# A fused attention and expert block: statistics of x moved among the first scores, and the attention of the last batch as products over 32 rows

## The chip, the cores and the metric

One core of a Trainium2 chip. The metric is the time of the device for one execution of the whole program, in microseconds (us). The program is written engine by engine: TensorE (PE), VectorE (DVE), ScalarE (ACT), GpSimd (POOL) and SyncE (SP, which only issues transfers) each have a fixed list of instructions, and semaphores join the lists.

## The reference

Four batches of 512 tokens, 128 values each, all in float32. An attention layer and a layer of eight experts (two of them weighted for each token) each stand between two normalisations and are added to x.

```python
x = x + layernorm(attention(layernorm(x)))
x = x + layernorm(ffn(layernorm(x)))

# attention, by batch:
probs = softmax(q @ k.T / sqrt(128)); out = probs @ v
# ffn, by token:
cont = sigmoid(h @ W_enc + b_enc) @ W_s2c + b_s2c        # 128 -> 256 -> 64
gate = two largest of softmax(cont @ Wr + br), scaled to a sum of 1
moe  = sum over 8 experts e of gate[e] * (relu(cont @ W1[e] + b1[e]) @ W2[e] + b2[e])
out  = layernorm(sigmoid(moe @ W_c2s + b_c2s) @ W_dec + b_dec) * ln_g + ln_b
```

## The kernel before

The 512 tokens of a batch b lie as four tiles t of 128 rows. `scores(b, t)` makes one tile's 128x512 scores in one of the two PSUM banks `ps_s`. VectorE takes the row maximum (`row_max`), ScalarE the exponentials with their row sums (`exps`), TensorE turns the tile's probabilities in four 128x128 blocks through its array (`turn_probs`, into `ps_t`), ScalarE copies them out (`pT_out`), and TensorE multiplies them with v, four products to a tile (`attend`, into `ps_o`). The row sums are never divided out: a normalisation follows, and the sums only scale its epsilon (`attn_var`). ScalarE sums the squares of the attention's output (`attn_squares`), GpSimd takes the power -1/2 (`inverse_std`), VectorE adds to x (`mid_stats`, which also takes the statistics of the sum) and normalises (`mid_norm`).

The experts follow: `encode`, `to_cont`, `route` on TensorE; `router_top`, `router_index`, `router_gates` on VectorE; the gates go through DRAM and come back spread over all partitions (`gate_out`, then SP's fetches); `hidden_pair` makes two experts' hidden layers, `gate_hidden` on VectorE does relu and gate for one expert, `expert_out` is the second product, `to_spikes` and `decode` the way back. `x_stats` and `x_norm` are statistics and normalisation of the input. Six small instructions on VectorE split a bias into bfloat16 pieces (`b_dec_hi` to `b_dec_stack`); `scaled_weights` centres the decoder's weights; both feed only the decoder.

The batches are pipelined by hand: while VectorE and ScalarE do the softmax of one batch, TensorE has the experts of an earlier one between. Nothing but these lists sets the order. Each engine takes its instructions strictly in turn, so an instruction that waits holds back all behind it.

Of the kernel before, what the change touches and what calls it, by code (L numbers as in the profile page):

```python
# [17 lines left out]
def attention_moe_block(  # L18
# [25 lines left out]
    out_dram = out.rearrange("b (p t) d -> b p t d", t=T)  # L44
    gates_dram = [nc.dram_tensor(f"gates{b}", [E, S], F32) for b in range(B)]

    with ExitStack() as ctx:
# [69 lines left out]
        x_out = sb("x_out", [P, B, T, D])  # L117
# [69 lines left out]
        ps_o = psum("ps_o", [P, 2, S])  # L187
        ps_c = psum("ps_c", [P, 2, S])
# [38 lines left out]
        def decoded_bank(b, t):  # L227
# [1329 lines left out]
```

## Time and profile before

| | us |
|---|---|
| three runs: median (lowest to highest) | 131.16 (130.88 to 131.32) |
| the profiled execution, its own time | 130.91 |
| span in its trace | 129.0 |
| TensorE busy | 118.7 (92% of the span) |
| VectorE busy | 94.4 (73%) |
| ScalarE busy | 58.8 (46%) |
| GpSimd busy | 33.8 (26%) |

The span runs from the first to the last instruction; 1.9 us of the execution's time lie around it. Busy time of TensorE counts overlapping products once, and also the time in which a product's end is still on its way through the array. A float32 product that isn't a transpose stands in the trace as two records.

### The profile page before, as it was taken

What the parts mean: (1) busy time and instruction counts of PE and PEld (TensorE: products, weight loads), DVE (VectorE), ACT (ScalarE), POOL (GpSimd) and SP (SyncE); (2) the same over time, 40 slices, a digit from 0 to 9 for tenths busy, and PEclk for the clock granted to TensorE, in tenths of its full rate; (3) what the DMA queues carried; (4) which work ended last, traced back from release to release, by engine and by line L of the source; (5) the groups of instructions that cost most, each with busy time, mean ns of one, the idle gap of its engine ahead of it and who ended that gap; (6) DMA issues with size and microseconds to landing.
All of it is one profiled execution on the core that took longest, in us unless ns stands there. A gap on an engine that the chain in (4) does not pass through costs nothing.

```text
span 129.0 us, 2501 instructions
## 1 busy us (share of the span) xinstructions
PE 118.7 (92%) x815; PEld 80.1 (62%) x815; DVE 94.4 (73%) x400; ACT 58.8 (46%) x173; POOL 33.8 (26%) x70
## 2 busy tenths in 40 slices
PE   6999999999999989999999999999998899998920
PEld 2556786878645767754575994657565455864910
DVE  0858537698989874788957168966889999389672
ACT  1647765556837575204666542053713003903620
POOL 4423503325231162220000132230081043330551
PEclk9999999999999999999999999999999999999998
DMA  3558800000000019700000198000019749720022
GB/s 113 132 121 227 234 18 3 0 0 3 0 5 0 0 50 324 290 8 0 0 0 0 41 293 329 3 0 0 8 48 319 299 138 323 276 86 0 4 79 81
DMA packets 9370, 12.42 MB, mean 96 GB/s; under 512 B 3169, under 2 KB 5998, under 8 KB 9358
## 3 DMA queue, kind: packets, MB, share of 16 engines
q1 hardware_dynamic: 8254, 12.08, 28.5%
q10 hardware_dynamic: 1104, 0.20, 0.8%
q8 instruction: 6, 0.10, 0.3%
q14 instruction: 6, 0.05, 0.1%
HBM read 11.16 MB, written 1.11 MB: 95 GB/s over the span
## 4 chain that ended last, share of the span: by engine, by line
PE 54%; DVE 23%; issue 8%; POOL 7%; ACT 3%; DMA 2%; POOLq 1%; DVEq 0%
PE ps_t L942 10%; POOL rstd L431 7%; PE ps_s L804 6%; PE ps_o L829 6%; PE ps_s L918 5%; PE ps_c L918 4%; DVE stats L1172 3%; PE ps_o L858 3%; PE ps_t L816 3%; DVE x_out L1366 2%; DMA x_in<-in_L_attn_x 2%; DVE xn L1184 2%; PE ps_o L918 2%; PE ps_a L769 2%; DVE neg_max L1200 2%
## 5 line engine op out<-in xcount | busy, mean ns | idle before, releaser
L431 POOL TENSOR_TENSOR rstd<-var_eps,minus_half 128x2 f32<-128x2 f32 (+1 forms) x33 | 25.4, 771 | 88.9 <-DVE var_eps L1177 47.3
L829 PEld LDWEIGHTS ps_o<-v,probsT 128*128 128x128 f32 x128 | 15.6, 191 | 4.6 <-ACT probsT L546 4.1
L829 PE MATMUL ps_o<-v,probsT 128*128 128x128 f32 x128 | 17.5, 279 | 0.4 <-ACT probsT L546 0.3
L942 PE MATMUL ps_t<-gated,w 128*64 128x256 f32 x128 | 17.0, 389 | 0.9 <-DVE gated L1286 0.8
L804 PE MATMUL ps_s<-xnT,yT 128*128 128x512 f32 x32 | 16.0, 596 | 0.1
L541 ACT ACTIVATE probs<-ps_s,neg_max 128x512 f32<-128x512 f32 x16 | 11.0, 687 | 11.1 <-DVE neg_max L1200 11.0
L1200 DVE TENSOR_REDUCE neg_max<-ps_s 128x1 f32<-128x512 f32 x16 | 10.9, 689 | 5.0 <-PE ps_s L804 4.9
L942 PEld LDWEIGHTS ps_t<-gated,w 128*64 128x64 f32 x128 | 8.0, 136 | 8.8 <-DVE gated L1286 4.2
L1286 DVE SCALAR_TENSOR_TENSOR gated<-ps_s,b_minus,gate_all 128x512 f32<-128x512 f32 x14 | 9.9, 744 | 1.9 <-PE ps_s L918 1.9
L546 ACT ACTIVATE probsT<-ps_t 128x512 f32<-128x512 f32 x16 | 9.5, 594 | 2.6 <-PE ps_t L816 2.4
L562 ACT ACTIVATE spikes<-ps_o,bias_half 128x512 f32<-128x512 f32 x6 | 4.1, 687 | 13.5 <-PE ps_o L858 13.4
L816 PE MATMUL ps_t<-ident,probs 128*128 128x128 f32 x64 | 9.8, 276 | 0.2 <-ACT probs L541 0.2
L816 PEld LDWEIGHTS ps_t<-ident,probs 128*128 128x128 f32 x64 | 7.3, 141 | 4.2 <-ACT probs L541 2.4
L1286 DVE SCALAR_TENSOR_TENSOR gated<-ps_c,b_minus,gate_all 128x512 f32<-128x512 f32 x12 | 8.4, 743 | 2.0 <-PE ps_c L918 2.0
L583 ACT ACTIVATE moeT<-ps_t 128x256 f32<-128x256 f32 x4 | 1.5, 384 | 14.5 <-PE ps_t L942 14.5
L918 PE MATMUL ps_s<-cont,w 64*128 64x256 f32 x56 | 7.9, 401 | 0.0
L804 PEld LDWEIGHTS ps_s<-xnT,yT 128*128 128x128 f32 x32 | 5.2, 191 | 2.7 <-issue 2.4
L1212 DVE SCALAR_TENSOR_TENSOR var_eps<-square_sum,eps_term 128x2 f32<-128x2 f32 x8 | 1.3, 165 | 7.1 <-ACT squares L552 6.9
L918 PE MATMUL ps_c<-cont,w 64*128 64x256 f32 x48 | 6.3, 380 | 0.0
L1219 DVE SCALAR_TENSOR_TENSOR x_mid<-ps_o,rstd,x_in 128x128 f32<-128x128 f32 x16 | 4.8, 343 | 2.0 <-POOL rstd L431 2.0
L918 PEld LDWEIGHTS ps_s<-cont,w 64*128 64x128 f32 x56 | 4.8, 186 | 2.1 <-issue 1.5
L1184 DVE TENSOR_SCALAR xn<-x_in,mean_var,rstd 128x128 f32<-128x128 f32 x16 | 5.2, 375 | 1.2 <-POOL rstd L431 0.9
(207 smaller groups left out, 218.6 us busy)
## 6 DMA issues: line engine op xcount, KB each, us to landing
gate_all<-gates SPq DMA_DIRECT2D x12, 512.0 KB, 6.0
gate_all<-gates SPq DMA_DIRECT2D x8, 256.0 KB, 3.6
x_in<-in_L_attn_x SPq DMA_DIRECT2D x3, 256.0 KB, 3.6
w<-in_L_ffn_W SPq DMA_DIRECT2D x3, 256.0 KB, 4.4
out<-x_out SPq DMA_DIRECT2D x3, 256.0 KB, 2.0
x_in<-in_L_attn_x SPq DMA_DIRECT2D x2, 128.0 KB, 2.5
out<-x_out SPq DMA_DIRECT2D x2, 128.0 KB, 1.7
w_enc<-in_L_ffn_W_enc SPq DMA_DIRECT2D x1, 128.0 KB, 2.7
```

Source lines behind the costliest of these rows:

```text
L431: nc.gpsimd.tensor_tensor(rstd[part], var_eps[part], minus_half[:, t0:t1], ALU.pow).then_inc(g_rstd[n], 1)
L541: nc.scalar.activation(probs[:, b % 2, t], ps_s[:, t % 2], ACT.Exp, bias=neg_max[:, b % 2, t:t + 1], accum_out=prob_sum[:, b % 2, t:t + 1] ...
L546: nc.scalar.activation(probsT[:, b % 2, t], ps_t[:, :].rearrange("p (k q) -> p k q", k=T), ACT.Identity).then_inc(a_pT, 1)
L804: nc.tensor.matmul(ps_s[:, t % 2], yT[:, b % 2, t * P:(t + 1) * P], xnT[:, b % 2], start=True, stop=True).then_inc(pe_s, 1)
L816: mm = nc.tensor.transpose(ps_t[:, k * P:(k + 1) * P], probs[:, b % 2, t, k * P:(k + 1) * P], ident[:, :])
L829: mm = nc.tensor.matmul(attn_out(t), probsT[:, b % 2, t, k], v[:, b % 2, k], start=(k == 0), stop=(k == T - 1))
L918: mm = nc.tensor.matmul(hidden_banks(b, e)[:, h], w1[half, e], cont[half, b % 2], start=True, stop=True)
L942: mm = nc.tensor.matmul(ps_t[h * M:(h + 1) * M, 0:SH], w2[:, e], gated[:, e, h * SH:(h + 1) * SH], start=False, stop=(e == E - 1))
L1184: nc.vector.tensor_scalar(result(t), source(t), mean_var[:, n, b % 2, t, 0:1], inv(n, b, t), ALU.subtract, ALU.mult).then_inc(done, 1)
L1200: nc.vector.tensor_reduce(neg_max[:, b % 2, t:t + 1], ps_s[:, t % 2], AX_X, ALU.max, negate=True).then_inc(v_max, 1)
L1219: nc.vector.scalar_tensor_tensor(x_mid[:, b, t], attn_out(t), inv(LN_ATT, b, t), x_in[:, b, t], ALU.mult, ALU.add).then_inc(v_mid, 1)
L1286: nc.vector.scalar_tensor_tensor(token_halves(gated[:, e]), hidden_banks(b, e), b1_minus[:, e:e + 1], token_halves(gate_all[:, b % 2, e]), ...
```

## The change

It has two parts and a new order around them.

1. `x_stats(2)` and `x_stats(3)` move from the middle of the attention of batches 1 and 2 to the first scores; the `x_norm` of both moves forward too. GpSimd's `inverse_std(LN_X, ...)` moves with them.
2. For batch 3 `turn_probs` and `pT_out` are gone. VectorE turns each probability tile in 32x32 blocks (`turn_blocks`: four transposes of 128x512). A block turned this way stays in its own 32 partitions, so the attention is summed as products over 32 rows: `attend_last` makes 64 products of 32 rows, 128 columns of weights and 129 columns of v, one partition group i of 32 after the other, each group with its own PSUM bank. For this v must be there for every key block in all four groups of partitions: SP writes v of batch 3 to DRAM and reads it back four times (`v_all`). The 129th column of v is one, so that the row sums come out of the products; the exponentials of batch 3 no longer sum. `yT` of batch 3 is written with its tokens permuted, so that the result has the rows in x's order. ScalarE copies the result out once (`att_out`, 128x516), and everything after reads the copy. The statistics of x_mid for batch 3 are squares summed on ScalarE (`mid_square`) about x's mean, in place of VectorE's bn_stats.
3. Order: `turn_x(2)` and `project_y(2)` stand earlier, the product behind `b_dec_sum` later; the six bias instructions move from batch 1's attention to behind the first two `turn_blocks`; all four scores of batch 3 now stand among the last expert products of batch 0, and `decode(0, ...)` is done before `attend_last`; `scaled_weights` stands behind the turned blocks; in front of the third expert round `z_stats` and `z_centre` of batch 0 stand ahead of `router_top(2)`, and the first two `gate_hidden(2, ...)` ahead of the last steps of the router of batch 3. `x_out` is gone: the result goes into `x_in`.

The diff, cut; the third piece stands in `hidden_pair`.

```diff
 for b in range(B):
+    if b == 1:
+        sp.wait_ge(g_v_ones, 1)
+        sp.wait_ge(a_v, B)
+        sp.dma_start(v_dram.ap(), v[:, (B - 1) % 2].rearrange("p t d -> p (t d)")).then_inc(d_v_out, 16)
+        sp.wait_ge(d_v_out, 16)
+        for i in range(T):
+            sp.dma_start(v_all[32 * i:32 * (i + 1)].rearrange("a j t d -> a j (t d)"),
+                         v_dram.ap().rearrange("(j a) x -> a j x", j=T)).then_inc(d_v_all, 16)
...
+def attend_last():
+    pe.wait_ge(v_blocks, T)
+    pe.wait_ge(d_v_all, 16 * T)
+    pe.wait_ge(v_mid, T * (B - 1))
+    pe.wait_ge(v_logit, 2)
+    pe.wait_ge(a_c2s, HC)
+    pe.wait_ge(v_gated, E)
+    for j in range(S // 32):
+        for i in range(T):
+            rows = slice(32 * i, 32 * (i + 1))
+            mm = nc.tensor.matmul(ps_oc[:, i, 0:D + 1], blocks[rows, j].rearrange("p t r -> p (t r)"),
+                                  v_all[rows, j % T, j // T], start=(j == 0), stop=(j == S // 32 - 1))
+    mm.then_inc(pe_o, 1)
...
     if b < 2:
+        if b == 1:
+            pe.wait_ge(a_exp, T * B)
         if p == 1:
+            if b == 1:
+                pe.wait_ge(a_att, 1)
+            pe.wait_ge(v_bdec, 1)
...
+def att_out():
+    act.wait_ge(pe_o, 2 * B - 1)
+    nc.scalar.activation(att[:, :, :], ps_oc[:, :, 0:D + 1], ACT.Identity).then_inc(a_att, 1)
+def mid_square(h):
+    b = B - 1
+    act.wait_ge(v_mid, T * b + TH * (h + 1))
+    for t in range(TH * h, TH * (h + 1)):
+        nc.scalar.activation(squares[:, b % 2, t], x_mid[:, b, t], ACT.Square, scale=-1.0,
+                             bias=mean_var[:, LN_X, b % 2, t, 0:1],
+                             accum_out=mid_square_sum[:, t:t + 1]).then_inc(a_mid_square, 1)
...
+def turn_blocks(t):
+    dve.wait_ge(a_exp, T * (B - 1) + t + 1)
+    dve.wait_ge(pe_o, 4)
+    nc.vector.transpose(blocks[:, :, t], probs[:, (B - 1) % 2, t]).then_inc(v_blocks, 1)
```

Three places show how rows move. First, TensorE's list from the last expert products of batch 0 (`ps_t<-gated,w`) to the first of batch 1. Before:

```order
L942 MATMUL ps_t<-gated,w 64x256 x8
L873 MATMUL ps_a<-spikes,w_s2c 64x256 x4
L954 MATMUL ps_c<-moeT,w_c2s 128x256 x4
L885 MATMUL ps_o<-w_r,cont 128x8 x4
L844 MATMUL ps_a<-ident,hn 128x128 x4
L816 MATMUL ps_t<-ident,probs 128x128 x4
L804 MATMUL ps_s<-xnT,yT 128x512
L829 MATMUL ps_o<-v,probsT 128x128 x4
L816 MATMUL ps_t<-ident,probs 128x128 x4
L804 MATMUL ps_s<-xnT,yT 128x512
L829 MATMUL ps_o<-v,probsT 128x128 x4
L816 MATMUL ps_t<-ident,probs 128x128 x4
```

The same place after the change (`xnT,yT` are the scores, `ident,hn` is `turn_h(2)`, `w_dec,spikes` is `decode(0, ...)`, `cont,w` is `hidden_pair(1, ...)`):

```order
L1010 MATMUL ps_t<-gated,w 64x256 x4
L852 MATMUL ps_s<-xnT,yT 128x512
L1022 MATMUL ps_oc<-moeT,w_c2s 128x256 x4
L852 MATMUL ps_s<-xnT,yT 128x512
L902 MATMUL ps_a<-ident,hn 128x128 x4
L1028 MATMUL ps_t<-b_dec_stack,ones_bf 128x512
L1068 MATMUL ps_t<-w_dec,spikes 128x128 x8
L889 MATMUL ps_oc<-v_all,probsT 128x129 x64
L983 MATMUL ps_s<-cont,w 128x256 x4
L983 MATMUL ps_oc<-cont,w 128x256 x4
```

The four turns and four attentions that alternated with other work are one run of 64 products, which needs all four tiles.

Second, VectorE's list between the third row maximum of batch 0 and the first of batch 1. Before:

```order
L1200 TENSOR_REDUCE neg_max<-ps_s 128x1
L1395 BN_STATS dec_stats<-w_dec_raw 128x6 x2
L1396 BN_STATS dec_stats<-b_dec_all 128x6
L1200 TENSOR_REDUCE neg_max<-ps_s 128x1
L1400 BN_AGGR dec_mean<-dec_stats 128x2 x2
L1401 BN_AGGR dec_mean<-dec_stats 128x2
L1208 SCALAR_TENSOR_TENSOR eps_term<-prob_sum 128x2
```

After:

```order
L1265 TENSOR_REDUCE neg_max<-ps_s 128x1
L1492 BN_STATS dec_stats<-w_dec_raw 128x6 x2
L1493 BN_STATS dec_stats<-b_dec_all 128x6
L1237 BN_STATS stats<-x_in 128x6 x4
L1240 BN_AGGR mean_var<-stats 128x2 x4
L1242 TENSOR_SCALAR var_eps<-mean_var 128x4
L1265 TENSOR_REDUCE neg_max<-ps_s 128x1
L1498 BN_AGGR dec_mean<-dec_stats 128x2 x2
L1499 BN_AGGR dec_mean<-dec_stats 128x2
L1237 BN_STATS stats<-x_in 128x6 x4
L1240 BN_AGGR mean_var<-stats 128x2 x4
L1242 TENSOR_SCALAR var_eps<-mean_var 128x4
```

Each of the two blocks of nine statistics instructions of batches 2 and 3 now stands on one side of the fourth row maximum.

Third, VectorE's list behind the turned blocks of batch 3 (`x_mid<-att` is `mid_add`, `gated` is `gate_hidden(1, ...)`); before, the first `gated` of this round stood directly behind `z<-ps_a,g_all`:

```order
L1432 TENSOR_SCALAR b_centred<-b_all,scaled_mean 128x128
L1278 SCALAR_TENSOR_TENSOR eps_term<-att 128x2
L1282 SCALAR_TENSOR_TENSOR var_eps<-square_sum,eps_term 128x2
L1294 SCALAR_TENSOR_TENSOR x_mid<-att,rstd,x_in 128x128 x2
L1278 SCALAR_TENSOR_TENSOR eps_term<-att 128x2
L1282 SCALAR_TENSOR_TENSOR var_eps<-square_sum,eps_term 128x2
L1383 SCALAR_TENSOR_TENSOR gated<-ps_s,b_minus,gate_all 128x512 x2
L1294 SCALAR_TENSOR_TENSOR x_mid<-att,rstd,x_in 128x128 x2
L1383 SCALAR_TENSOR_TENSOR gated<-ps_oc,b_minus,gate_all 128x512
```

`gate_hidden(1, 0)` now has the whole first half of the attention's normalisation ahead of it on its engine.

## Rows read from the trace of the kernel before

**Rows 1.** The page, top and part 1: engine, busy us, share, instructions.

```profile
span 129.0 us, 2501 instructions
PE 118.7 (92%) x815; PEld 80.1 (62%) x815; DVE 94.4 (73%) x400; ACT 58.8 (46%) x173; POOL 33.8 (26%) x70
```

**Rows 2.** One window: length, busy us of PE, PEld, DVE, ACT, POOL; clock; DMA.

```profile
76.50:88.40 11.90, 11.89 (x86) 6.73 (x85) 9.41 (x27) 4.00 (x16) 2.78 (x4) 1.00 0.30 110
```

**Rows 3.** TensorE's timeline, from route(0) to hidden_pair(0, 0): start, us, what, [idle before].

```profile
36.58 0.62 PE L885 MATMUL ps_c<-w_r,cont 64*128 64x8 f32 x8
...
51.93 1.14 PE L918 MATMUL ps_s<-cont,w 64*128 64x256 f32 x8
52.90 1.03 PE L918 MATMUL ps_c<-cont,w 64*128 64x256 f32 x8
```

**Rows 4.** VectorE's timeline, the places that the moved statistics leave and take.

```profile
16.49 0.69 DVE L1200 TENSOR_REDUCE neg_max<-ps_s 128x1 f32<-128x512 f32 x1 [1.77 <-PE ps_s L804]
...
19.11 0.16 DVE L1212 SCALAR_TENSOR_TENSOR var_eps<-square_sum,eps_term 128x2 f32<-128x2 f32 x1 [1.67 <-ACT squares L552]
...
33.92 0.22 DVE L1435 CAST b_dec_hi<-b_dec_sum 128x128 bf16<-128x128 f32 x1
...
35.50 0.16 DVE L1208 SCALAR_TENSOR_TENSOR eps_term<-prob_sum 128x2 f32<-128x2 f32 x1
...
43.40 0.86 DVE L1172 BATCH_NORM_STATS2 stats<-x_in 128x6 f32<-128x128 f32 x4
```

**Rows 5.** TensorE's timeline, the attention of batch 3 and what surrounds it.

```profile
62.03 1.95 PE L942 MATMUL ps_t<-gated,w 128*64 128x256 f32 x16
...
65.74 0.51 PE L885 MATMUL ps_o<-w_r,cont 64*128 64x8 f32 x8
66.18 0.66 PE L844 MATMUL ps_a<-ident,hn 128*128 128x128 f32 x4
...
70.71 1.16 PE L829 MATMUL ps_o<-v,probsT 128*128 128x128 f32 x8 [0.29 <-ACT probsT L546]
...
73.25 1.06 PE L829 MATMUL ps_o<-v,probsT 128*128 128x128 f32 x8
74.14 0.60 PE L816 MATMUL ps_t<-ident,probs 128*128 128x128 f32 x4
74.58 1.06 PE L1002 MATMUL ps_a<-w_dec,spikes 128*128 128x128 f32 x8
...
76.52 1.13 PE L918 MATMUL ps_s<-cont,w 64*128 64x256 f32 x8
```

**Rows 6.** Groups by line and form: count, busy us, mean ns of one.

```profile
L1200 DVE TENSOR_REDUCE neg_max<-ps_s 128x1 f32<-128x512 f32 x16 | 10.9, 689 | 5.0 <-PE ps_s L804 4.9
L1277 DVE STREAM_TRANSPOSE gate_blocks<-gate 128x32 f32<-128x32 f32 x4 | 0.8, 212 | 0.1
L1263 DVE TENSOR_SCALAR e_sum<-e 128x4 f32<-128x4 f32 x4 | 0.7, 162 | 0.0
```

**Rows 7.** ScalarE's and VectorE's timelines, batch 3's first half normalised, then gated hidden layers.

```profile
72.83 0.27 ACT L552 ACTIVATE squares<-ps_o 128x128 f32<-128x128 f32 x1
...
73.56 0.16 DVE L1212 SCALAR_TENSOR_TENSOR var_eps<-square_sum,eps_term 128x2 f32<-128x2 f32 x1 [2.34 <-ACT squares L552]
74.53 0.61 DVE L1219 SCALAR_TENSOR_TENSOR x_mid<-ps_o,rstd,x_in 128x128 f32<-128x128 f32 x2 [0.81 <-POOL rstd L431]
...
77.70 0.75 DVE L1286 SCALAR_TENSOR_TENSOR gated<-ps_s,b_minus,gate_all 128x512 f32<-128x512 f32 x1 [1.02 <-PE ps_s L918]
```

**Rows 8.** TensorE's timeline from route(2) on, and its last group.

```profile
88.40 0.62 PE L885 MATMUL ps_o<-w_r,cont 64*128 64x8 f32 x8
...
97.04 1.13 PE L918 MATMUL ps_o<-cont,w 64*128 64x256 f32 x8 [0.61 <-DVE logits L1232]
...
100.46 1.31 PE L942 MATMUL ps_t<-gated,w 128*64 128x256 f32 x8 [0.84 <-DVE gated L1286]
...
106.72 1.14 PE L918 MATMUL ps_s<-cont,w 64*128 64x256 f32 x8
```

More of the change, by code:

```diff
@@ new lines, in _ @@
+            pe.wait_ge(v_wdec, 8)
+            pe.wait_ge(v_logit, 1)
+            for c in range(HC):
+                mm = nc.tensor.matmul(ps_c[:, 0, 0:D], ones[:, :], w_dec[:, c], start=(c == 0), stop=(c == HC - 1))
+            mm.then_inc(pe_bdec, 1)
+            turn_probs(2, 0)
+            scores(2, 2)
+            attend(2, 0)
+            turn_probs(2, 1)
+            turn_h(1)
+            scores(2, 3)
+            attend(2, 1)
+            turn_probs(2, 2)
+            turn_x(3)
+            attend(2, 2)
@@ new lines, in _ @@
+            turn_probs(2, 3)
+            project_y(3)
+            attend(2, 3)
+            project_v(3)
+            hidden_pair(0, 0)
+            hidden_pair(0, 1)
+            expert_biases(0)
+            for e in range(4):
+                expert_out(0, e)
+            hidden_pair(0, 2)
+            hidden_pair(0, 3)
+            encode(1, 0)
+            encode(1, 1)
+            scores(3, 0)
+            scores(3, 1)
+            to_cont(1)
+            expert_out(0, 4)
+            expert_out(0, 5)
@@ new lines, in _ @@
+            route(1)
+            expert_out(0, 6)
+            expert_out(0, 7)
+            scores(3, 2)
+            to_spikes(0)
+            scores(3, 3)
+            turn_h(2)
+            for t in range(T):
+                decode(0, t)
+            attend_last()
+            hidden_pair(1, 0)
+            hidden_pair(1, 1)
+            expert_biases(1)
+            for e in range(4):
+                expert_out(1, e)
+            hidden_pair(1, 2)
+            hidden_pair(1, 3)
+            encode(2, 0)
@@ L1491, in _ @@
             gate_hidden(1, 7)
-            dec_var(0, 0)
             z_scale(0, 0)
+            z_stats(0, 0)
+            z_centre(0)
             router_top(2)
@@ L1496, in _ @@
             router_gates(2)
-            z_stats(0, 0)
-            z_centre(0)
             z_add(0, 0)
@@ L1503, in _ @@
             router_index(3)
-            router_gates(3)
-            for e in range(6):
+            router_weights(3)
+            gate_hidden(2, 0)
+            gate_hidden(2, 1)
+            router_blocks(3)
+            for e in range(2, 6):
                 gate_hidden(2, e)
```

360 lines of the change are left out of this document (178 added, 182 removed).

## The prediction

> **What bounds the kernel now.** I read the page first, then the windows, then the timelines of the engines. TensorE is busy for 118.7 of 129.0 us [rows 1], and between 76.5 and 88.4 without a gap, at the full clock (1.00, the level of 2.4 GHz) [rows 2]. So the end moves with TensorE: by the products that it no longer makes, and by the waits that it gains or loses. A busy TensorE hides small waits, however. Each step has a pace that shows where nothing holds it: four attention products (eight records) take 0.89 us (73.25 to 74.14), four turns 0.44 (74.14 to 74.58) [rows 5]. From `route(0)` at 36.58 to `hidden_pair(0, 0)` at 51.93 it takes 15.35 us [rows 3] for work worth some 12.7: four scores of 0.86, four turns, four attentions, and 4.0 us of projections, turns of x and h, and routing. About 2.6 us are late answers of VectorE and ScalarE. In the attention of batch 3 (66.18 to 76.52) 10.3 us hold 5.3 us of turning and attending [rows 5].
>
> All times below are in the frame of this trace. The profiled execution took 130.91 us, 1.9 more than its span; the median of the runs shown is 131.16, so I add 0.25 at the end.
>
> **First statistics.** Each `x_stats` is 1.35 us of VectorE (43.40 on: four of bn_stats, four aggregates, one more) [rows 4]. VectorE idles 1.77 us ahead of the fourth row maximum of batch 0 and 1.67 us ahead of 19.11, waiting for squares [rows 4]. If x has landed, both blocks fit there and cost nothing; if that cover were gone, each would push a row maximum by up to 1.35. Landing is my estimate: the loads for batches 2 and 3 are issued at 10.5 and 13.4 us by SP and land in some 3.6, so by 14.1 and 17.0, while VectorE gets to them at 14.7 and 17.4. The norm of batch 2 (1.1 us) goes into a similar gap near 23.5.
>
> What leaves the middle: 1.35 us ahead of the last row maximum of batch 2, 1.35 at 29, and the six bias instructions, 33.92 to 35.50, 1.6 us [rows 4]. I followed the lists from `route(0)`: with y of batch 2 projected earlier, scores(2, 2) starts 0.9 earlier, the last row maximum 1.0 earlier, turn_x(3) 1.2, and `hidden_pair(0, 0)` at 50.5 in place of 51.93, after the 0.44 of the product behind b_dec_sum, which now lies in this stretch. **Term 1: -1.4.** Bounds: 0 (a single late answer remains) and -2.2 (2.6 less 0.44).
>
> **The attention of batch 3.** From 62.03 TensorE has left: experts 4 to 7 (1.8), to_cont 1.0, route 0.44, two scores 1.7, to_spikes 1.0, turn_h 0.5, decode(0) 2.0. That is 8.4 us and replaces 14.5 less 5.3 of turns and attentions (some 0.8 of the 14.5 was waiting, 0.29 of it at 70.71 [rows 5]).
>
> The price of `attend_last` is not in the trace. A record of 128 columns over the full array comes every 111 ns (0.89 over 8) [rows 5]; 128 records in a row would be 14.2 us. But products over 64 rows run two at a time: `hidden_pair` makes 8 records of 256 columns in 0.97 us (51.93 to 52.90) [rows 3], 121 ns each, when the full array's pace would be 222. Their weight loads go in pairs too: in route 8 records, each with 128 columns of weights, take 0.44 us (65.74 to 66.18), 55 ns each [rows 5]. So with pairs only it is 7.2 us, with four at a time 32 steps of 112 ns, 3.6. The list rotates over the four groups, each with its own bank, as route's and hidden_pair's do over two, so I take 3.6 and 0.2 for its start: 3.8. The Trainium skill weighs against this: "TensorE: Matmul & The Clock Gate", Part 3 (measured speedup), gives 3.07 times for four products of 32 rows, not four. By that it would be an estimated 14.2/3.07 = 4.6 us, 0.8 more; no row here shows four.
>
> What it waits for: the last `turn_blocks`. A 128x512 reduction on VectorE takes 689 ns. The transposes seen are 128x32, 212 ns, against 162 for an operation of 4 columns [rows 6]: 50 ns for 28 columns more would be 1.8 ns a column, 1.0 us for 512; if it streams as the reduction does, 0.69. I take 0.69, nearest in size (in a row 0.6, since starts overlap ends); the other end adds 0.3 twice before the router of batch 1 and twice after, 1.2 in all. The Trainium skill, "Vector Engine (DVE) Microarchitecture Reference", 3.8, has the transpose sustain one element per cycle per lane, which would be the short one.
>
> Followed through, still without term 1: blocks 0 and 1 and the bias pieces end at 65.7, router_top(1) to its weights at 67.7, row maximum 68.3, router_blocks 69.2, row maximum 69.85, exponential 70.55, block 3 done 71.3. `decode(0)` waits for the second `spike2(0, ...)`, now behind an exponential, and runs 69.8 to 71.8; TensorE idles 1.3 before it. The transposes are thus just hidden. The attention runs 71.8 to 75.6, against hidden_pair(1, 0) at 76.52 [rows 5]. **Term 2: -0.9.** v_all's data (1 MB, issued after 51) lands by 62 and isn't late.
>
> **Behind the attention.** Here a wait is added. hidden_pair(1, 1) waits for att_out (0.6 us on ScalarE plus 0.2 to be noticed), about covered by the 0.97 of hidden_pair(1, 0). But gate_hidden(1, 0) is now queued behind attn_var(3, 0), mid_add(3, 0) and attn_var(3, 1), and expert_out(1, 0), with all of TensorE's list behind it, waits for it. From the attention's end: 0.85 copy, 0.5 squares (before: first square at 72.83, var_eps at 73.56), 1.0 from var_eps to x_mid (73.56 to 74.53), 0.6 x_mid, 0.2 attn_var, then 0.7 for the gate [rows 7]: expert_out(1, 0) starts 4.1 after the end. Before, gate_hidden started at 77.70, 1.2 after 76.52 [rows 5, 7]. Then VectorE paces the first four experts (four gates of 0.67, 0.6 of mid_add, small ones): expert 3 at 6.85, hidden_pair(1, 2) 7.3 to 8.25, and the encoders, turn_h(3), the last experts and to_cont(2) follow at their pace, with route(2) 14.25 after the end. Before it was 11.88 (76.52 to 88.40) [rows 5, 8]. **Term 3: +2.35.** Nothing but the end of the DVE list hides it, since VectorE is filled by scaled_weights only until just before. Its bounds: 0 if the first experts were as quick as before, +3.5 if POOL's powers for LN_MID hold mid_norm(3, 1) another 1.1.
>
> **The last third.** route(2) comes at -1.4 - 0.9 + 2.35 = 0.05 after 88.40. Behind it VectorE had 97.04 held up by 0.61 and 100.46 by 0.84 [rows 8]. With z_stats and z_centre (2.1 us) taken out from between routers 2 and 3, the logits of batch 3 are taken as soon as they exist: hidden_pair(2, 2) starts 0.35 earlier. With router_blocks(3) behind gate_hidden(2, 0), expert_out(2, 0) starts 1.0 earlier. The router's last steps (0.8) then delay gates 2 to 5 of this round, and of the 1.0 some 0.7 to 0.75 are left at 106.72 [rows 8]. From there to its last product TensorE waits little, so the rest shifts. **Term 4: -0.75** (0 to -1.4, all of both waits).
>
> Sum: -1.4 - 0.9 + 2.35 - 0.75 = -0.7. 130.91 - 0.7 = 130.2, plus 0.25: **130.4 us** against 131.16.
>
> **Rivals.**
> - *The four row groups do not pack as two do* (their loads or the order of issue are shared). Pairs only: +3.4, 133.8, chance 0.10. The middle between pairs and four, 5.4 us: +1.6, 132.0, chance 0.07. For it: no four are seen here. Against: every pair in the trace overlaps in loads and products. By the skill's 3.07 it would be +0.8, 131.2, between this and the forecast. Beyond 4.5 us of attention the change no longer pays.
> - *Slow transposes*, the one that ends on the other side by one mechanism on VectorE: 1.0 us each puts the attention 1.2 later, nothing takes it back, 131.6; chance 0.15. It decides from 0.2 us over my price per transpose.
> - *The front gains nothing*, because another late answer (ScalarE's copies between TensorE's steps) takes the place of VectorE's: +1.4 on the sum, 131.8; chance 0.13. For it: ScalarE copies between nearly all of TensorE's steps here. Against: each step that I followed had its predecessors.
> - *The hand-over is cheaper than term 3* by a microsecond: 129.4; chance 0.10.
> - The forecast, 130.4 with 129.7 to 131.0 as its own range: chance 0.45.
>
> **How the numbers follow.** 0.3% (about what a measurement of this kernel can tell) is 0.4 us: faster means below 130.77, slower above 131.55. Faster: 0.10 + 0.38 of the forecast's 0.45 + 0.03 of the front's = 0.51. Slower: 0.17 of the packing + 0.08 of the transposes + 0.06 of the front = 0.31. The same: 0.07 + 0.07 + 0.04 of these three (forecast, transposes, front) = 0.18. For the range I leave out the pairs (0.10) and the ends of the others: 129.1 to 132.5, which takes in both prices of the transpose and the middle of the packing.
>
> **What would show it.** attend_last as 128 records within 3.6 to 4 us; transposes of 0.7; `hidden_pair(0, 0)` near 50.5; route(1), ahead of the last scores, near 62.6; the attention ending near 74.2; TensorE idle for about 1.7 us ahead of expert_out(1, 0), and smaller gaps behind it with VectorE named; route(2) near 88.4; hardly any wait for logits at 96.7. The prediction is wrong if the attention's records come more than 35 ns apart, if row_max(0, 3) starts later than 16.6 because x had not landed, if SP's transfers of v stand in front of gates that are needed, or if TensorE's gaps behind the attention let its clock fall to the lower level (1.2 GHz), of which the trace of before has no case until its products are over.

## The result

The changed kernel takes 134.28 us (median of 6 runs, 132.26 to 136.04) against 131.03 (130.85 to 132.65): slower, and outside my range of 129.1 to 132.5. Its ratio to the kernel before is 1.0159, 95% interval 1.0095 to 1.0223 (the ratio leaves out runs more than 1.5% above the fastest). The profiled execution took 134.0, with a span of 132.2.

The top of its page, part 1, and the row of part 2 with the granted clock in 40 slices, answer to [rows 1]:

```profile
span 132.2 us, 2668 instructions
PE 121.2 (92%) x895; PEld 79.6 (60%) x895; DVE 94.6 (72%) x396; ACT 58.8 (45%) x174; POOL 33.7 (26%) x71
...
PEclk9999999999999999999999999599999999999996
```

The 5 in the 26th slice is new: in the middle of the program TensorE ran at half its clock for a while. Three windows of the changed kernel, from the attention's end on (length, busy us of PE, PEld, DVE, ACT, POOL, clock, DMA share, GB/s), answer to [rows 2]:

```profile
78.96:80.96 2.00, 0.68 (x6) 0.20 (x4) 1.32 (x5) 0.86 (x6) 1.01 (x2) 1.00 0.98 397
80.96:84.96 4.00, 3.56 (x16) 1.12 (x16) 3.55 (x11) 1.05 (x6) 2.04 (x4) 0.64 0.26 101
84.96:88.96 4.00, 4.00 (x23) 2.48 (x22) 2.57 (x6) 0.67 (x1) 2.72 (x8) 0.94 0.00 0
```

TensorE works only 0.68 of 2 us, waiting for gates; then the granted clock is 0.64 and 0.94 on the mean of two windows in which it is busy. By these two rows it is at the lower of its two levels, 1.2 GHz, for 3.4 us.

TensorE's timeline of the changed kernel (start, us, what, [idle before]); from its third row on it answers to [rows 3, 5, 8]:

```profile
9.72 2.21 PE L852 MATMUL ps_s<-xnT,yT 128*128 128x512 f32 x4
...
17.15 1.02 PE L852 MATMUL ps_s<-xnT,yT 128*128 128x512 f32 x2
...
53.13 1.14 PE L983 MATMUL ps_s<-cont,w 64*128 64x256 f32 x8
...
71.18 0.38 PE L1028 MATMUL ps_t<-b_dec_stack,ones_bf 128*128 128x512 bf16 x1 [0.77 <-ACT spikes L639]
...
73.28 3.85 PE L889 MATMUL ps_oc<-v_all,probsT 32*128 32x129 f32 x128
77.06 1.13 PE L983 MATMUL ps_s<-cont,w 64*128 64x256 f32 x8
...
81.25 1.69 PE L1010 MATMUL ps_t<-gated,w 128*64 128x256 f32 x8 [1.61 <-DVE gated L1383]
...
92.25 0.61 PE L945 MATMUL ps_oc<-w_r,cont 64*128 64x8 f32 x8
...
109.94 1.14 PE L983 MATMUL ps_s<-cont,w 64*128 64x256 f32 x8
```

And the same places at the start of the kernel before:

```profile
8.32 1.88 PE L804 MATMUL ps_s<-xnT,yT 128*128 128x512 f32 x4
...
15.43 1.02 PE L804 MATMUL ps_s<-xnT,yT 128*128 128x512 f32 x2
```

Three things stand in these rows. The first scores already come at 9.72 instead of 8.32 and take 2.21 instead of 1.88, though no instruction of TensorE's was changed up to there: the products run at half pace until about 10.4 us (the first scores take 0.33 us more, which is some 0.7 us at half pace behind 9.72). The attention itself is 3.8 us long (73.28 to 77.06), as costed. And `route(2)` stands at 92.25, 15.2 us behind the attention's end, where it was 11.88 [rows 5, 8].

VectorE behind the attention answers to [rows 7]:

```profile
77.83 0.16 DVE L1278 SCALAR_TENSOR_TENSOR eps_term<-att 128x2 f32<-128x2 f32 x1 [1.65 <-ACT att L587]
78.63 0.16 DVE L1282 SCALAR_TENSOR_TENSOR var_eps<-square_sum,eps_term 128x2 f32<-128x2 f32 x1 [0.64 <-ACT squares L604]
79.60 0.61 DVE L1294 SCALAR_TENSOR_TENSOR x_mid<-att,rstd,x_in 128x128 f32<-128x128 f32 x2 [0.81 <-POOL rstd L458]
...
80.44 1.41 DVE L1383 SCALAR_TENSOR_TENSOR gated<-ps_s,b_minus,gate_all 128x512 f32<-128x512 f32 x2
```

And two groups by line and form, to [rows 6]:

```profile
L889 PE MATMUL ps_oc<-v_all,probsT 32*128 32x129 f32 x128 | 3.9, 274 | 0.0
...
L1289 DVE STREAM_TRANSPOSE probsT<-probs 128x512 f32<-128x512 f32 x4 | 2.8, 706 | 0.3
```

A transpose of 128x512 takes 706 ns, close to the 0.69 that I took and far from 1.0.

### The profile page after: what moved, and what is told of

It is laid out like the page before. It is cut to its first block, busy times and chain, and to the rows that moved or that the text cites. A ratio compares the mean times of both kernels' runs of the same rounds, so it can differ in the third digit from the quotient of the medians.

```text
span 132.2 us, 2668 instructions
## 1 busy us (share of the span) xinstructions
PE 121.2 (92%) x895; PEld 79.6 (60%) x895; DVE 94.6 (72%) x396; ACT 58.8 (45%) x174; POOL 33.7 (26%) x71
## 4 chain that ended last, share of the span: by engine, by line
PE 69%; DVE 14%; ACT 5%; issue 4%; POOL 3%; DMA 2%; POOLq 1%; ACTq 0%; DVEq 0%
PE ps_t L1010 9%; PE ps_s L852 8%; PE ps_oc L873 7%; PE ps_oc L918 6%; PE ps_s L983 5%; PE ps_oc L983 4%; PE ps_t L862 4%; PE ps_oc L889 3%; POOL rstd L458 3%; PE ps_a L825 2%; ACT probs L577 2%; PE ps_a L835 2%; DMA w_qkv<-in_L_attn_Wk 2%; PE ps_t L1068 2%; DVE neg_max L1265 2%
## 5 line engine op out<-in xcount | busy, mean ns | idle before, releaser
L1383 DVE SCALAR_TENSOR_TENSOR gated<-ps_oc,b_minus,gate_all 128x512 f32<-128x512 f32 x18 | 12.6, 741 | 2.1 <-PE ps_oc L983 2.1
L873 PE MATMUL ps_oc<-v,probsT 128*128 128x128 f32 x96 | 13.1, 279 | 0.2 <-ACT probsT L582 0.2
L873 PEld LDWEIGHTS ps_oc<-v,probsT 128*128 128x128 f32 x96 | 11.7, 192 | 2.7 <-ACT probsT L582 2.7
L614 ACT ACTIVATE spikes<-ps_oc,bias_half 128x512 f32<-128x512 f32 x8 | 5.5, 688 | 13.6 <-PE ps_oc L918 13.5
L983 PE MATMUL ps_oc<-cont,w 64*128 64x256 f32 x72 | 9.5, 388 | 0.3 <-DVE logits L1321 0.3
L862 PEld LDWEIGHTS ps_t<-ident,probs 128*128 128x128 f32 x48 | 5.4, 141 | 4.3 <-ACT probs L577 2.5
L918 PE MATMUL ps_oc<-hT,w_enc 128*128 128x512 f32 x16 | 7.8, 612 | 0.0
L983 PEld LDWEIGHTS ps_oc<-cont,w 64*128 64x128 f32 x72 | 6.6, 187 | 1.9 <-issue 0.4
L862 PE MATMUL ps_t<-ident,probs 128*128 128x128 f32 x48 | 7.3, 276 | 0.3 <-ACT probsT L582 0.3
L582 ACT ACTIVATE probsT<-ps_t 128x512 f32<-128x512 f32 x12 | 7.1, 592 | 0.8 <-PE ps_t L862 0.6
```

What stands on the lines that cost most here:

```text
L582: nc.scalar.activation(probsT[:, b % 2, t], ps_t[:, :].rearrange("p (k q) -> p k q", k=T), ACT.Identity).then_inc(a_pT, 1)
L614: nc.scalar.activation(spikes[:, b % 2, c], enc_bank(b, c), ACT.Tanh, bias=bias_half[:, c:c + 1], scale=0.5).then_inc(a_enc, 1)
L862: mm = nc.tensor.transpose(ps_t[:, k * P:(k + 1) * P], probs[:, b % 2, t, k * P:(k + 1) * P], ident[:, :])
L873: mm = nc.tensor.matmul(attn_out(t), probsT[:, b % 2, t, k], v[:, b % 2, k, 0:D], start=(k == 0), stop=(k == T - 1))
L918: nc.tensor.matmul(enc_bank(b, c), w_enc[:, c * P:(c + 1) * P], hT[:, b % 2], start=True, stop=True).then_inc(pe_enc, 1)
L983: mm = nc.tensor.matmul(hidden_banks(b, e)[:, h], w1[half, e], cont[half, b % 2], start=True, stop=True)
```

## The experiments

Five points cut each trace into stretches that can be compared whatever the start did: `scores(0, 3)`, `hidden_pair(0, 0)`, `hidden_pair(1, 0)` (the attention's end), `route(2)`, and `decode_scaled`'s first product with `w_z`. Times in us, each the difference of two starts on TensorE's timeline:

| trace | scores(0, 3) at | to hidden_pair(0, 0) | to hidden_pair(1, 0) | to route(2) | to decode_scaled |
|---|---|---|---|---|---|
| before | 15.43 | 36.50 | 24.59 | 11.88 | 32.91 |
| changed, first | 17.15 | 35.98 | 23.93 | 15.19 | 32.28 |
| changed, rerun (a1) | 15.20 | 35.99 | 23.93 | 14.39 | 32.91 |
| zeros in the gap (a2) | 15.05 | 35.98 | 23.93 | 14.75 | 33.24 |
| gates first (a3) | 15.67 | 35.98 | 23.93 | 13.55 | 33.39 |
| statistics back (b1) | 15.32 | 35.98 | 23.93 | 14.39 | 32.69 |
| old last third (b2) | 15.34 | 35.98 | 23.93 | 14.39 | 32.75 |
| gates of batch 1 sent early (d2) | 15.51 | 35.80 | 23.93 | 12.15 | 33.19 |
| no fetch, changed (f1) | 15.70 | 35.99 | 23.94 | 15.73 | 32.29 |
| no fetch, best order (f2) | 15.47 | 35.79 | 23.94 | 12.63 | 32.35 |

Among kernels with the same order there, the first two stretches repeat to 0.01 us. The others vary, by the clock and by a transfer, as the runs show.

**a1_again: nothing changed.** 

> The changed kernel, unaltered. Its six runs so far spread from 132.26 to 136.04, in step with their mean granted clock (0.988 to 0.967), and its trace has 3.4 us at 1.2 GHz behind the attention and reaches full pace of the products at 10.4 us instead of 4.8. Theory (the clock): the times fall into levels about 1.7 us apart, by how many such stretches a run has; the mean granted clock goes down by 0.013 with each (3.4 us at half of 132), and the late start, which the mean clock does not show, is chance: in this trace it can come at 4.8 or at 10.4. Rival (the schedule itself is slower): times within 0.5% at whatever clock.

133.45 us (131.89 to 135.38), ratio 1.0155 (1.0079 to 1.0231). This trace has neither the lower clock in the middle nor the late start, and the execution took 131.89, 1.0 above the profiled one of before. It is the schedule by itself. From the stretches: -0.23 at the start, -0.51, -0.66, +2.51, 0.00, in all +1.11 on TensorE. The first trace has +1.72, -0.52, -0.66, +3.31, -0.63, in all +3.22. The mean clock told of the middle (0.968 to 0.988), but levels 1.7 us apart were not to be seen: one run took 135.30 us at 0.986, which neither the clock in the middle nor one late start accounts for. Two executions of the kernel before are like it (134.25 and 134.39 at 0.990 and 0.989); they stay unexplained.

**a2_fill: products of zeros in the gap.** 

> Products of zeros into a free bank, eleven of 128 x 512 bf16, stand where TensorE waits for the gates behind the attention (seven ahead of expert_out(1, 0), four between the experts); nothing else is changed. Clock theory: TensorE has no gap there, the granted clock stays 1.00 until the last products, every run has the mean clock of 0.985 or more, and the median falls by 1.3 to 2 us, to 132.3 to 133. Rival 1 (the attention over 32 rows, not the gap, lowers the clock): the drop stays, the time stays 134 or gets worse. Rival 2 (the drop costs nothing, as VectorE paces the experts): the clock holds and the time stays within 0.4 us.

```diff
 expert_biases(1)
+fill(7)                       # matmul(ps_o[:, 0], zeros[:, 0:P], zeros)
 for e in range(4):
     expert_out(1, e)
+    fill((1, 2, 1, 0)[e])
```

132.42 us (132.36 to 133.85), ratio 1.0140 (1.0073 to 1.0206). No run had a mean clock under 0.987, where the changed kernel had 0.967 to 0.980 in 7 of 12. So it is the gap that brings the lower clock; d1 below shows it from the other side. The trace shows the price of the zeros too: `route(2)` 14.75 behind the attention's end, 0.36 more than in a1.

**a3_gates: four gates ahead of the norm.** 

> VectorE's list behind the attention only: gate_hidden(1, 0) to (1, 3) ahead of mid_add(3, 0), with both attn_var(3, ...) between the second and third gate. My step (the hand-over, +2.35 us, is there because the gates are queued behind the norm of batch 3): expert_out(1, 0) starts about 1.9 us after the attention's end instead of 4.2, route(2) within 12.5 us of it instead of 15.2, and the time falls by 2 to 3 us, to 131 to 132. With the gap smaller the clock should hold as well. Rival (the norm of batch 3, now later, becomes the late one at turn_h(3)): TensorE waits as long there and route(2) stays near 14.5.

```diff
+gate_hidden(1, 0)
+gate_hidden(1, 1)
 attn_var(3, 0)
-mid_add(3, 0)
 attn_var(3, 1)
-gate_hidden(1, 0)
-gate_hidden(1, 1)
-mid_add(3, 1)
 gate_hidden(1, 2)
-mid_var(0)
 gate_hidden(1, 3)
+mid_add(3, 0)
+mid_add(3, 1)
+mid_var(0)
 dec_var(0, 0)
```

131.61 us (130.25 to 133.97), ratio 1.0007 (0.9968 to 1.0047). `expert_out(1, 0)` starts 2.4 behind the end instead of 4.2, so the queue on VectorE is the cause of that first wait. But `route(2)` gains only 0.84 of the 2.51. TensorE and then VectorE in that kernel:

```profile
77.99 1.03 PE L1010 MATMUL ps_t<-gated,w 128*64 128x256 f32 x8
80.12 1.31 PE L1010 MATMUL ps_t<-gated,w 128*64 128x256 f32 x8 [1.10 <-DVE gated L1383]
...
85.80 0.66 PE L902 MATMUL ps_a<-ident,hn 128*128 128x128 f32 x4 [0.52 <-DVE hn L1312]
```

```profile
79.32 1.41 DVE L1383 SCALAR_TENSOR_TENSOR gated<-ps_oc,b_minus,gate_all 128x512 f32<-128x512 f32 x2 [0.60 <-DMA gate_all<-gates]
...
101.08 0.75 DVE L1383 SCALAR_TENSOR_TENSOR gated<-ps_s,b_minus,gate_all 128x512 f32<-128x512 f32 x1 [1.02 <-DMA gate_all<-gates]
```

The next late thing is the transfer of the rows of gates (VectorE's first row here), and then the norm, for which TensorE waits 0.52 (the rival, in part). VectorE's second row lies behind `route(2)`, where the rows are late as well.

**a4_unpacked: one row group after the other.** 

> attend_last with its two loops exchanged: the 32 products of one row group, then those of the next, each with its own bank as before. If the four groups overlap because their products alternate, none does now: 128 records at 111 ns, 14.2 us for the attention instead of 3.8, and the time near 144. If the order doesn't matter: 3.8 us and 134.

```diff
-for j in range(S // 32):
-    for i in range(T):
+for i in range(T):
+    for j in range(S // 32):
```

148.51 us. The attention on TensorE's timeline, then three windows inside it:

```profile
71.58 20.58 PE L889 MATMUL ps_oc<-v_all,probsT 32*128 32x129 f32 x128
```

```profile
72.00:76.00 4.00, 4.00 (x41) 4.00 (x40) 2.42 (x13) 1.14 (x8) 0.00 (x0) 1.00 0.79 222
...
77.30:80.00 2.70, 2.70 (x19) 2.70 (x18) 0.00 (x0) 0.00 (x0) 0.00 (x0) 0.50 0.65 264
80.00:85.00 5.00, 5.00 (x26) 5.00 (x26) 0.00 (x0) 0.00 (x0) 0.00 (x0) 0.50 0.01 5
```

At the full clock the records come every 111 ns, as said. But TensorE, busy without a gap inside the attention, was put to the lower clock 5.7 us into the attention and stayed there to its end: 20.5 us instead of 14.2. Alternating groups make 128 records in 3.78 us, 29.5 ns each, 3.8 times the pace of one group at full clock.

**b3_pairs: two row groups at a time.** 

> attend_last for two row groups at a time: the 64 products of groups 0 and 1 alternating, then those of 2 and 3. One group at a time took 111 ns a record at full clock and fell to 1.2 GHz after 5.7 us. If groups overlap as far as they alternate: 64 steps of 112 ns, 7.2 us, at full clock; the attention is then 3.4 longer than the 3.78 of four. If the array counts as busy only by the rows in use, the clock falls inside it or just behind, and it takes 8 or more; time 137 to 139.

```profile
71.28 7.08 PE L890 MATMUL ps_oc<-v_all,probsT 32*128 32x129 f32 x128
```

134.92 us. 7.0 us to the next product, as costed, at full clock. Groups overlap as far as they alternate.

**b1_stats_back: the statistics of term 1 put back.** 

> The changed kernel with x_stats(2), x_norm(2), x_stats(3) and x_norm(3), and POOL's powers for them, back at their old places among batches 1 and 2; TensorE's and ScalarE's new order stays. In the rerun of the changed kernel the stretch from scores(0, 3) at 15.20 to hidden_pair(0, 0) at 51.19 took 35.99 us, before 36.50: a gain of 0.5 where I had forecast 1.4. My step (VectorE's statistics were the late answers, and something took back 0.9): the stretch gets 0.9 to 1.6 us longer than 35.99, and the time rises by as much. Rival (row_max(2, 2) behind the router's steps of batch 0, at 42.60 in both kernels, and ScalarE's copies of the turned probabilities hold this stretch): it stays within 0.4 of 35.99.

```diff
-x_stats(2)
 row_max(0, 3)
 ...
-x_stats(3)
 attn_var(0, 0)
 ...
 row_max(2, 2)
+x_stats(3)
 row_max(2, 3)
+x_norm(3)
```

133.0 us (131.8 to 134.36), and the stretch is 35.98, the same to 0.01: the moved statistics are worth nothing. My term 1 is wrong, and the rival holds. The last two row maxima of batch 2 on VectorE, in the kernel before:

```profile
42.80 0.68 DVE L1200 TENSOR_REDUCE neg_max<-ps_s 128x1 f32<-128x512 f32 x1
...
45.01 0.69 DVE L1200 TENSOR_REDUCE neg_max<-ps_s 128x1 f32<-128x512 f32 x1 [0.26 <-PE ps_s L804]
```

And in the rerun (a1), with the waits of TensorE's weight loads for ScalarE's copies between 36 and 52 us (us in all, times, longest):

```profile
42.60 0.68 DVE L1265 TENSOR_REDUCE neg_max<-ps_s 128x1 f32<-128x512 f32 x1
...
44.69 0.69 DVE L1265 TENSOR_REDUCE neg_max<-ps_s 128x1 f32<-128x512 f32 x1 [1.40 <-PE ps_s L852]
```

```profile
PEld ps_oc L873 <- ACT probsT L582: 2.7, 4, 0.8
```

The third row maximum, behind the router's steps, comes 27.4 us behind `scores(0, 3)` in both. The fourth comes 0.1 earlier, where I had forecast 1.0: the time that the statistics left became a wait of VectorE for TensorE's scores. TensorE's loads wait 2.7 us for the copies there (2.3 before). That the copies hold the stretch fits this; no run made them faster. The 0.5 us that the stretch did gain comes with the new order of the lists around it, whose parts were not taken apart.

**b2_old_tail: VectorE's order of term 4 undone.** 

> The changed kernel with the old order of VectorE's last third: z_stats(0, 0) and z_centre(0) behind the router of batch 2, and the router of batch 3 undivided ahead of gate_hidden(2, 0). My step: from route(2) to hidden_pair(3, 1) it takes 18.3 us, as before, instead of 17.7 in the first trace of the changed kernel; expert_out(2, 0) 12.0 behind route(2) instead of 11.0. The rerun, however, took 18.33 for the stretch, with three waits of VectorE for the rows of gates (gate_all), 0.9 us in all. Rival (the new order only moves VectorE ahead of the transfer of these rows): no waits for gate_all here, and the stretch is 18.3 in any case, so the order is worth 0 to 0.7 by how quick the transfer is.

```diff
+router_top(2), router_index(2), router_gates(2)
 z_stats(0, 0)
 z_centre(0)
-router_top(2), router_index(2), router_gates(2)
 ...
-router_weights(3)
-gate_hidden(2, 0), gate_hidden(2, 1)
-router_blocks(3)
-for e in range(2, 6):
+router_gates(3)
+for e in range(6):
```

133.6 us (131.86 to 136.39). `expert_out(2, 0)` comes 11.87 behind `route(2)` instead of 11.0, and still the whole stretch is 32.75, between the two of the changed kernel. VectorE waited for no rows until gate 6 (0.75). In the rerun it had waited three times:

```profile
100.74 0.75 DVE L1383 SCALAR_TENSOR_TENSOR gated<-ps_s,b_minus,gate_all 128x512 f32<-128x512 f32 x1 [0.29 <-DMA gate_all<-gates]
...
103.71 1.41 DVE L1383 SCALAR_TENSOR_TENSOR gated<-ps_oc,b_minus,gate_all 128x512 f32<-128x512 f32 x2 [0.16 <-DMA gate_all<-gates]
...
105.69 1.41 DVE L1383 SCALAR_TENSOR_TENSOR gated<-ps_s,b_minus,gate_all 128x512 f32<-128x512 f32 x2 [0.42 <-DMA gate_all<-gates]
```

**f1_no_fetch and f2_no_fetch_best: the fetch taken away.** 

> The changed kernel, in which SP fetches no rows of gates for batches 2 and 3: their experts are weighted with the rows of batches 0 and 1, which are still there (that part of the result is left out). If the fetch is what took term 4 back, VectorE waits nowhere for gate_all behind route(2), the stretch from route(2) to the last product group takes 32.3 us or less, against 32.91 in the kernel before, and the median falls by 0.3 to 1.0 from 133.45 to 134.28. If something else on VectorE paces it, the stretch stays at 32.9.

> The same left out of d3_gates1_fill, whose 12 runs stood in two heaps, 129.8 to 130.1 and 130.9 to 131.7. If the late rows of batches 2 and 3 make the second heap, it is gone: all runs but late starts at or below 130.1, within 0.3 of each other. If the heaps stay, they come from elsewhere (the rows of batch 1, or the start).

```diff
 sp.wait_ge(d_gate_out[b], 16)
 if b >= 2:
-    sp.wait_ge(v_gated, E * (b - 1))
-    sp.wait_ge(pe_moe, b - 1)
+    continue
```

f1: 131.91 us (131.31 to 133.11), with 32.29 for the last stretch. The kernel before has no wait of VectorE for the rows behind `route(2)` in its trace, so this is about the order's own worth, -0.62 against 32.91: term 4 (-0.75) was nearly right. The fetch takes nothing of it in the first trace of the changed kernel and all of it in the rerun, and in a2 and a3, with the same order there, 0.3 and 0.5 more than all. f1's ten runs also price the clock: five with a mean clock of 0.990 or more stand at 131.3 to 131.6, five at 0.978 to 0.980 at 132.3 to 133.1, 1.3 us higher on the mean. f2: 129.66 us, ratio 0.9893 (0.9882 to 0.9904); ten of 12 runs lie between 129.46 and 129.92. d3's second heap (below) is gone, so the late rows, or `gateT` that is fetched with them, made it.

**c3_before_gap and d1_before_gap_long: a gap behind the old attention.** 

> The kernel before, with four additions on 128 x 512 put ahead of gate_hidden(1, 0) on VectorE, whose result nobody reads: expert_out(1, 0) comes 2.0 us later and TensorE waits about 1.7 us, as in the changed kernel, but behind the old attention over 128 rows. Theory (any gap of this length there can bring the lower clock): a part of the runs, a third to two thirds, have 3.4 us at 1.2 GHz, with a mean clock under 0.985 and a time 0.8 to 1.7 above the rest; the rest near 133. Rival (the attention over 32 rows is needed for it, as in the run with one group at a time, where the clock fell while it ran): no run under 0.985, all within 0.5 of 133 or 1.6 above with a late start.

> The kernel before with six additions ahead of gate_hidden(1, 0) instead of four: TensorE's gap behind the old attention over 128 rows becomes about 2.4 us, against 1.1 with four and 1.6 in the changed kernel. If a gap of this length is enough to bring the lower clock, a good part of the runs has 3.4 us of it (mean clock under 0.985) and spreads up by 1 to 2 us from 133.5. If the 32-row attention ahead of the gap has a part in it, no run is under 0.985, as with four.

```diff
 dec_scale(0, 0)
+for k in range(4):                     # d1: range(6)
+    tensor_tensor(idle, x_in[:, 0], x_in[:, 0], ALU.add)
 gate_hidden(1, 0)
```

c3: 132.22 us (131.54 to 133.67), no run of 7 under 0.985; its gap was only 1.1 us. d1: 134.35 us (133.37 to 135.52), 5 of 6 runs at 0.976 to 0.981. Its trace (TensorE, then a window):

```profile
81.90 3.62 PE L944 MATMUL ps_t<-gated,w 128*64 128x256 f32 x16 [2.54 <-DVE gated L1288]
```

```profile
82.00:84.00 2.00, 2.00 (x10) 0.92 (x12) 2.00 (x4) 0.00 (x0) 0.70 (x1) 0.50 0.00 0
```

So the products over 32 rows are not needed for it; the gap is enough, if it is long. Runs with a mean clock under 0.985, by the longest gap there:

| gap, us | kernels | such runs |
|---|---|---|
| none | before (the runs beside a to f) | 0 of 120 |
| 0.4 to 0.6 | d2, b4 | 0 of 20 |
| 1.1 to 1.5 | a3, c1, c2; c3 | 3 of 36; 0 of 7 |
| 1.6 | changed kernel, b1, b2, f1 | 16 of 30 |
| 2.5 | d1 | 5 of 6 |
| filled with zeros | a2, d3, f2; e1 | 0 of 30; 1 of 12 |

**b4_best, c1_relisted, c2_gate_out_early, d2_gates1_early, d3_gates1_fill: towards a better order.** 

> The order of VectorE from the run with the gates first, and three more moves: row_max(2, 2) between router_weights(0) and router_blocks(0), mid_norm(3, 1) ahead of gate_hidden(1, 4), and SP fetches the first two experts' rows of gates ahead of gateT. Theory (row_max(2, 2) was 0.85 late behind the router, turn_h(3) waited 0.52 for hn, the rows of gates are the late transfer): hidden_pair(0, 0) 0.4 to 0.8 sooner behind scores(0, 3) than 35.99, no wait for hn at turn_h(3), the waits for gate_all shorter by 0.3; time 130.0 to 131.0, below before's 131.07 by 0.3 to 1. Rival (ScalarE's copies bound the stretch, the transfers are late anyway): as the run with the gates first, 131.6.

> As the run with three more moves, but SP's transfers in their old order (gateT first), and POOL takes both powers of LN_MID of batch 3 ahead of that of LN_DEC, with dec_var(0, 0) behind mid_var(1). In the last run expert_biases(2) waited 1.54 us for gateT, and the second mid_norm waited 1.04 for POOL, with TensorE idle 0.40 ahead of turn_h(3). Theory: route(2) 13.0 us after the attention's end instead of 13.41, no wait for gateT, so 0.4 and about 1.0 off 132.03: 130.5 to 131.0, at or just below before's 131.08. Rival (the rows of gates come as late as before, at random by a microsecond): 131.0 to 132 with a spread of one.

> As c1_relisted, with gate_out(2) on ScalarE between spike(3, 0) and spike(3, 1). In the changed kernel the rows of gates of batch 2 lie ready at 93.1 and are sent at 93.9, behind both. If their way (send, fetch, land) is what ends the gain of the last third, they land 0.4 sooner and the waits of VectorE for gate_all shrink by as much: time 0.2 to 0.4 below c1_relisted. Rival (the way is quick or slow at random, and 0.4 doesn't show): the same within 0.3.

> As c2_gate_out_early, with gate_out(1) ahead of exps(3, 3) on ScalarE. There the rows of gates of batch 1 were ready at 70.0 and sent at 70.8, and VectorE waited 0.70 for them ahead of gate_hidden(1, 2) (0.98 in c1_relisted). If their way bounds it, they land 0.5 sooner and route(2) comes 12.3 to 12.6 behind the attention's end instead of 12.94; time 130.4 to 131.0, 0.4 below c2's 131.26 and at or under before. If they land late by chance: 131.3.

> As d2_gates1_early, with five products of zeros in TensorE's remaining gap ahead of expert_out(1, 2). One run in twelve of each gates-first kernel still fell under a mean clock of 0.985. With the gap filled none does; the time of the others is that of d2 within 0.3, or up to 0.4 above it where the gap is shorter than the fillers.

```diff
 router_weights(0)                      # VectorE, b4 on
+row_max(2, 2)
 router_blocks(0)
-row_max(2, 2)
 ...
 inverse_std(LN_MID, 3, 0)              # POOL, c1 on
-inverse_std(LN_DEC, 0, 0)
 inverse_std(LN_MID, 3, 1)
+inverse_std(LN_DEC, 0, 0)
 ...
 mid_norm(3, 0)                         # VectorE, b4 on
+mid_norm(3, 1)
 gate_hidden(1, 4)
 gate_hidden(1, 5)
-mid_norm(3, 1)
 ...
 spike(3, 0)                            # ScalarE, c2 on
+gate_out(2)
 spike(3, 1)
-gate_out(2)
 ...
+gate_out(1)                            # ScalarE, d2 on
 exps(3, 3)
-gate_out(1)
 ...
 expert_out(1, 1)                       # TensorE, d3
+fill(5)
 expert_out(1, 2)
```

| kernel | median us (lowest to highest) | ratio, 95% interval |
|---|---|---|
| b4 | 132.03 (131.45 to 132.25) | 1.0067 (1.0044 to 1.0089) |
| c1 | 131.54 (129.81 to 133.68) | 0.9995 (0.9967 to 1.0024) |
| c2 | 131.26 (130.29 to 134.5) | 1.0001 (0.9980 to 1.0022) |
| d2 | 131.18 (129.74 to 134.58) | 0.9978 (0.9945 to 1.0012) |
| d3 | 130.99 (129.79 to 133.32) | 0.9974 (0.9943 to 1.0005) |

b4's early row maximum gave 0.2 us to the first stretch, not 0.4 to 0.8, which fits that something behind VectorE holds it. Its other transfer order was a mistake: behind two fetches the 16 KB of `gateT` came so late that TensorE waited 1.54 us for them.

```profile
100.67 0.65 PE L1005 MATMUL ps_t<-gateT,b_plus 128*64 128x256 f32 x4 [1.54 <-DMA gateT<-gates]
```

In c1 and c2 the rows of batch 1 were late by 0.98 and 0.70 ahead of `gate_hidden(1, 2)`. d2, which sends them sooner, had no such wait, and `route(2)` 12.15 behind the attention's end. d2 and d3 stand in two heaps (d3: five runs at 129.8 to 130.1, five at 130.9 to 131.7). No order that computes everything beats the kernel before beyond its interval.

**e1_warm_new and e2_warm_before: the start.** 

> As d3_gates1_fill, with a seventh warm-up product of zeros ahead of the first fold and another one behind fold_v, where TensorE waited 0.51 us for the first norm. If gaps between the first products bring the late start, no run has it: none above 132, the median 130.3 to 130.8. If it is chance that these gaps don't touch: one or two of 12 runs at 133 again, and the median 131.0. Each product costs 0.43 us at the lower clock, of which all but some 0.3 lies in waits.

> The kernel before with the same two products. If they cost nothing: 131.05 within 0.3; if they delay the first fold, 131.3. Late starts (132.6 and more) were 6 of 82 here, too few for this run to tell; it is the control for e1_warm_new, whose gain over d3 should show only where starts were late.

```diff
-WARM_UP = 6
+WARM_UP = 7
 ...
 fold_v()
+warm_up(1)
```

e1: 131.04 us (130.62 to 132.71), ratio 0.9985 (0.9948 to 1.0021); e2: 131.29 us (130.82 to 131.66), ratio 1.0011 (0.9985 to 1.0038). None of these 24 executions is 1.5 us or more late at a mean clock over 0.985 (e1's 132.71 has 0.981), against 12 of the 120 of the kernel before whose clock is on record; at that rate 2 or 3 of 24 would be expected. That suggests that the gaps have a part in the late start, but doesn't show it; e1 gained nothing in the median, its trace having 33.97 in the last stretch.

## Why the prediction was wrong

By its own steps:

- **Term 1, -1.4: it failed.** This is the first step that failed: the wait that I had wrong. The stretch gained 0.51, and with the statistics put back (b1) it gains the same. I took VectorE's instructions for the late answers because they stood there and the sum of late time was 2.6 us. But batch 2's third row maximum is behind the router's steps in both kernels, and the fourth, which I had 1.0 earlier, came 0.1 earlier, with VectorE idle for 1.40 us ahead of it until its scores came. What remains as the late answer are ScalarE's copies of the turned probabilities, for which TensorE's loads wait 2.7 us there; no run tested that alone. This was my rival "the front gains nothing", with 0.13; it was nearly so. At their new place the statistics of batch 2 waited 0.65 us for x in the rerun, where I had counted on none, and the fourth row maximum of batch 0 came at 16.39 (16.6 in the frame of before, which has 16.49); by b1 that cost nothing.
- **Term 2, -0.9: right, -0.66.** The attention's 3.78 us are as costed, pairs too (7.0). The 0.24 missing lies ahead of it and is not the transposes'. In the rerun the last two end at 70.60, 0.7 us before the attention, which follows `decode(0)` at once (VectorE, then TensorE):

```profile
69.06 1.54 DVE L1289 STREAM_TRANSPOSE probsT<-probs 128x512 f32<-128x512 f32 x2
```

```profile
69.24 0.38 PE L1028 MATMUL ps_t<-b_dec_stack,ones_bf 128*128 128x512 bf16 x1 [0.77 <-ACT spikes L639]
...
71.33 3.85 PE L889 MATMUL ps_oc<-v_all,probsT 32*128 32x129 f32 x128
```

In the forecast's frame (0.74 later, as `hidden_pair(0, 0)` is) the decoding starts at 69.98 against my 69.8, held by ScalarE's `spikes`, and the attention at 72.07 against 71.8. The page "TensorE: Matmul & The Clock Gate" of the Trainium skill, Part 3, with 3.07 times for products of 512 columns, does not fit this kernel, whose products of 129 columns have 3.8.

- **Term 3, +2.35: right, +2.51** at full clock, and by the mechanism named: `expert_out(1, 0)` 4.2 behind the end (4.1 foretold), `hidden_pair(1, 2)` 7.3 (7.3); a3 takes 1.8 of this hand-over away, though only 0.84 of it reaches `route(2)`.
- **The clock: a term put at nothing.** I listed the fall to 1.2 GHz under what would make the prediction wrong and gave it no chance. It came in 7 of 12 runs, for 0.8 us in the first trace and 1.34 in f1's, and a2 and d1 show that it hangs on the gap of term 3.
- **Term 4, -0.75: right as an order (-0.62 in f1), but 0 to -0.63 in the kernel.** The step that failed is a wait left out. I followed VectorE's list and not the rows that it needs. They are sent 4.4 us behind `route(2)` in both kernels, and VectorE now comes for them about 1.1 us sooner.
- **The start.** The first trace's 1.7 us at the start is not the change's: TensorE's list there is the same in both kernels, and the rerun has -0.23. c3's trace has it too, with the list of the kernel before up to that place: its first scores stand at 9.71 and `scores(0, 3)` at 17.19.

Sum of the rerun: -0.51 - 0.66 + 2.51 + 0.00 = +1.34, against my -0.7. Of the 2.0 between them 0.9 is term 1, 0.75 term 4 and 0.4 the small misses of terms 2 and 3. With +1.34 my sum would have been 132.5, the edge of my range; what lies beyond, up to the medians of 133.45 and 134.28, I put down to the clock in the middle and late starts, without a trace of each run to show it.

## What to carry to other kernels

A late answer is found by following one chain back through every engine, not by adding up one engine's idle time; the test is to put the step back where it was. A reordering that brings a consumer forward needs the same look at the transfer that feeds it: here 0.6 us of it came and went with the fetch. And a new gap on an engine that was always busy is priced twice, once as the wait, once for the clock behind it.

## What the runs showed of the hardware

- Where TensorE had a gap of 1.6 us between busy stretches, 16 of 30 executions had a mean clock under 0.985; with 2.5 us 5 of 6, with 1.5 and less 3 of 63, with products of zeros in the gap 1 of 42. The three traces of such executions (the changed kernel's first, f1's and d1's) show 3.4 us at 1.2 GHz behind the gap. The length of the gap is that of each kernel's one trace.
- Products over 32 rows in one row group at a time, without any gap, were put to the lower clock after 5.7 us and stayed there to the attention's end (a4, one run). Two or four groups in turn, in 7.0 and 3.8 us, did not bring it in their traces.
- The moment at which TensorE first reaches full pace is not fixed: 4.1 us in the rerun of the changed kernel, 10.4 in its first trace, the same instructions. "TensorE: Matmul & The Clock Gate" in the Trainium skill, Part 1, has the transition vary from run to run too, by about half a microsecond either way; here it was over six. The row of granted clocks in the page stands at full there in both traces; the length of the first products shows it.
